# Waits behind groups of GpSimd scatters and gathers in a macaron block with a mixture of experts

## The reference

```python
def reference(x, ...):
    x = x + 0.5 * _L0_ffn_ref(_layernorm(x), ...)
    x = x + _L0_attn_ref(_layernorm(x), ...)
    x = x + 0.5 * _L0_ffn_ref(_layernorm(x), ...)
    return x

def _forward(x, ...):                       # the feed-forward step
    xn = (x - mu) * rsqrt(var + EPS) * ln_gamma + ln_beta
    abel_out = gelu(xn @ abel_w + abel_b)
    topw, topi = top_k(xn @ moe_gate_w + moe_gate_b, 2)      # 2 of 8 experts
    w_dense = sum(one_hot(topi, 8) * softmax(topw)[..., None], axis=-2)
    h = gelu(einsum('bsd,edh->ebsh', xn, ew1) + eb1)         # 128 -> 256
    moe_out = einsum('ebsd,bse->bsd', einsum(h, ew2) + eb2, w_dense)
    for i in range(3):
        moe_out = moe_out @ expm(gens[i])
    gate = sigmoid(concatenate([abel_out, moe_out]) @ gc_w + gc_b)
    return x + abel_out * (1.0 - gate) + moe_out * gate
```

## Time and profile before

| | |
|---|---|
| time, median of 3 runs | 788.86 us (786.06 to 794.77) |
| span of the profiled execution, first to last instruction | 883.8 us |
| TensorE busy | 683.1 us (77%) |
| VectorE busy | 568.2 us (64%) |
| GpSimd busy | 485.6 us (55%) |
| ScalarE busy | 410.8 us (46%) |
| mean granted TensorE clock | 0.913 |

### The profile page before, as it was taken

One profiled execution on the slowest core, in us unless ns is written; L12 is line 12 of the kernel. 1 busy time (PEld: TensorE's weight loads), 2 busy tenths in 40 slices (PEclk: granted clock), 3 DMA queues, 4 the chain that ended last, 5 costly groups with the idle time before them and its releaser, 6 DMA issues.

```text
span 883.8 us, 16149 instructions
## 1 busy us (share of the span) xinstructions
PE 683.1 (77%) x4719; PEld 492.3 (56%) x4719; DVE 568.2 (64%) x1922; ACT 410.8 (46%) x931; POOL 485.6 (55%) x588
## 2 busy tenths in 40 slices
PE   1465667979897798997988979999997777838760
PEld 1355656979793354654646545455544466837750
DVE  3675545968767876876767767787673235745538
ACT  2243411545560265664545645556554655615530
POOL 2656554034512666576866768373645466566661
PEclk9968777988898899998999999999997999969985
DMA  8614544744348313023050240302201235233525
GB/s 242 205 48 117 132 123 115 183 112 105 94 113 192 110 31 98 18 65 87 2 130 21 49 103 1 98 17 55 61 13 53 85 78 167 75 93 84 175 96 154
DMA packets 89825, 84.04 MB, mean 95 GB/s; under 512 B 14561, under 2 KB 72556, under 8 KB 89580
## 3 DMA queue, kind: packets, MB, share of 16 engines
q1 hardware_dynamic: 74472, 57.51, 25.8%
q0 software_dynamic: 8800, 19.72, 7.5%
q10 hardware_dynamic: 6468, 5.79, 2.8%
HBM read 43.84 MB, written 31.13 MB: 85 GB/s over the span
## 4 chain that ended last, share of the span: by engine, by line
PE 46%; DVE 15%; another core or an unknown queue 11%; issue 7%; ACT 7%; SPq 5%; ACTq 3%; DMA 3%; POOL 1%; DVEq 0%; POOLq 0%
PE bank L2361 6%; PE bank L2271 6%; PE bank L2401 6%; PE bank L2286 6%; PE bank L2426 6%; SPq L595 4%; DVE mx_of L1923 3%; PE pair L2449 2%; PE bank L2363 2%; ACT beside_parts L1254 2%; DMA qT<-mT_zero 2%; PE pair L2213 2%; PE bank L2246 1%; ACT arena L1326 1%
## 5 line engine op out<-in xcount | busy, mean ns | idle before, releaser
L1326 ACT ACTIVATE arena<-bank 128x512 f32<-128x512 f32 x320 | 184.0, 599 | 175.2 <-PE bank L2401 147.1
L1923 DVE TENSOR_REDUCE mx_of<-bank 128x4 f32<-128x512 f32 x320 | 204.2, 684 | 81.9 <-PE bank L2361 42.9
L2401 PE MATMUL bank<-qT,kZ 128*128 128x512 f32 (+3 forms) x512 | 156.9, 377 | 19.2 <-ACT arena L1326 12.4
L975 POOL TENSOR_SCALAR_AFFINE_SELECT arena<-arena 128x256 f32<-128x256 f32 (+1 forms) x192 | 95.4, 521 | 123.9 <-ACT arena L1326 122.5
L2361 PE MATMUL bank<-kZ,qT 128*128 128x512 f32 x320 | 148.5, 481 | 15.7 <-DVE mx_of L1923 6.2
L2401 PEld LDWEIGHTS bank<-qT,kZ 128*128 128x128 f32 x512 | 95.7, 197 | 49.2 <-ACT arena L1326 24.1
L868 POOL DMA_INDIRECT z_rows<-beside_kZ,place x80 | 78.7, 984 | 51.5 <-DVE place L1685 29.8
L2361 PEld LDWEIGHTS bank<-kZ,qT 128*128 128x128 f32 x320 | 63.1, 200 | 70.7 <-issue 31.4
L885 POOL DMA_INDIRECT sums<-y_rows,y_place x56 | 54.4, 971 | 84.9 <-DMA y_rows<-arena 70.0
L2426 PE MATMUL bank<-arena,vA 128*9 128x512 f32 (+3 forms) x1024 | 92.4, 440 | 5.2 <-POOL arena L975 2.7
L1254 ACT ACTIVATE beside_parts<-bank,hidden_bias 128x128 f32<-128x128 f32 x160 | 45.5, 381 | 69.6 <-remote 44.0
(11 more groups left out here) (286 smaller groups left out, 1306.7 us busy)
## 6 DMA issues: line engine op xcount, KB each, us to landing
arena<-z_rows SPq DMA_DIRECT2D x128, 66.0 KB
qT<-parts SPq DMA_DIRECT2D x42, 128.0 KB
kZ<-parts SPq DMA_DIRECT2D x168, 32.0 KB
y_rows<-arena SPq DMA_DIRECT2D x20, 264.0 KB, 3.3
kZ<-bias_k_r SPq DMA_DIRECT2D x8, 512.0 KB
beside_kZ<-y_rows SPq DMA_DIRECT2D x7, 528.0 KB, 3.9
z_rows<-in_spare SPq DMA_DIRECT2D x4, 528.0 KB
z_rows<-in_spare SPq DMA_DIRECT2D x32, 66.0 KB
```

What stands on the lines that cost most here:

```text
L975: g_.affine_select(out=cut, in_=cut, compare_op=ALU.is_ge, fill=0.0, base=0, pattern=[[0, 2], [0, blocks], [1, P]], channel_multiplier=-1) ...
L1326: a_(dst, src, ACT.Exp).then_inc(exp_ok.sem, 1)
L1923: v.tensor_reduce(mx_of[:, queries, :, t, keys], ps_a[n % NA][:, :].rearrange("p (q n) -> p q n", q=NQ), AX.X, ALU.max).then_inc(reduced.s ...
L2401: return mm(outp, kZ[u][:, h, lo:lo + P], qT[u][:, t, lo:SEQ], start=start, stop=True, skip_group_check=(kind != "full"))
```

## The change

In send_z, GpSimd counts the scatters of a chunk that it has issued. For the chunks of the set-up (g below 8) it waits after the third and after the sixth until all that were issued have landed. In gather, for the chunks 0 and 1 of layer 0, it waits after the second, fourth, sixth and eighth gather in the same way. Everything else is as it was.

```diff
+SET_UP_GROUP, EARLY_GROUP = 3, 2
...
             def send_z(g, picks=(0, 1), tiles=range(NT)):
                 run = run_of_chunk(*divmod(g, CH))
                 wait(pool, placed, g)
                 z_done(pool, g)
+                sent = 0
                 for k in picks:
                     for t in tiles:
                         g_.indirect_dma_start(z_rows[run], bass.IndirectOffsetOnAxis(place[g % DEEP][:, k, t:t + 1], 0),
                                               zz(g)[:, k, t, :], None).then_inc(z_sent[g % DEEP], 16)
+                        sent += 1
+                        if g < CH and sent % SET_UP_GROUP == 0:
+                            pool.wait_ge(z_sent[g % DEEP], 16 * sent)
...
+                got = 0
                 for k in picks:
                     for t in tiles:
                         g_.indirect_dma_start(terms(0, c)[0][:, t, k, :], None, y_rows[run],
                                               bass.IndirectOffsetOnAxis(y_place[:, c, k, t:t + 1], 0)
                                               ).then_inc(sums_in[1 if c == 1 else 0], 16)
+                        got += 1
+                        if c < 2 and got % EARLY_GROUP == 0:
+                            pool.wait_ge(sums_in[c], 16 * got)
```

## The result

| | before | changed |
|---|---|---|
| median of 4 runs | 788.52 us | 835.64 us |
| lowest to highest | 786.06 to 794.77 | 835.52 to 836.70 |
| ratio | 1 | 1.059, 95% interval 1.056 to 1.063 |
| span of the profiled execution | 883.8 us | 833.8 us |

The change makes the kernel 47 us slower, 5.9%. The profiled execution of the changed kernel took 835.52 us, 1.7 us more than its span. Taking a profile does not by itself add 95 us, then; whether the unchanged kernel does so whenever it is profiled is the question of e1. They answer to the earlier trace rows.

The account below looks back on a forecast made before the run. TensorE held 46% of the chain; 99 us of unknown waits were taken as mostly profile-only. Set-up 1.0, gathers 3.2, less 1.8 us saved, gave +2.4 us on 788.9: 791.3 us, range 770 to 804.

Parts of the forecast that it names:

- So in the profiled execution an engine can be held until GpSimd's pile of indirect DMAs has landed.: Set-up and gathers: idle VectorE and ScalarE restart about when the pile's last transfer lands; 99 us of unknown waits in all.
- what goes: Set-up, experts of layer 0, gathers: a tenth of the unknown waits is 3.7 us; shorter runs save half, 1.8 us.
- the holes are real in the timed runs too: Rival: unknown waits in set-up and gathers also exist unprofiled, so the change saves 17 us, 771.5 us; chance 0.33.
- The sign that the prediction had named for its reading: Whole kernel: unknown waits belong to the profile if the span falls by 10 us or more and the time does not.
- Set-up, the price of a wait, 1.45 us: GpSimd's scatters: each wait for landing adds 1.45 us over the 0.30 us gap, with ends 1.3 and 2.85 us.
- Set-up, the deadline: Before quad 6: scatters must land by 145.1 us in timed runs; they land 0.5 us late, taken as 1 us.
- the waits turn late: Rival: at 1.9 us a wait, quad 6 and both gathers' gates come late, 12.3 us together, 801.2 us; chance 0.31.
- Gathers: Chunks 0 and 1 of layer 0: chunk 0 costs about nothing, chunk 1 shows 3.2 us beyond ScalarE's slack.
- is not added twice: attention_norm(0): VectorE's wait for the roots, and TensorE's behind it, fall at about the gathers' 3.2 us, adding nothing.
- The Trainium skill's rule: DMA queues: engines serve both descriptor kinds round robin, so scatters hold nobody back and waits only cost, +4.2 us.

Follow-up runs that it names:

- e1: The kernel before, unchanged, profiled once more: ratio 1.0005, span 788.0 us.
- e7: Kernel before plus only the 16 set-up waits, with SyncE's key-row loads moved behind the loads of quads 6 to 14: 813.02 us, ratio 1.030.
- e3: Kernel before plus only the 8 waits of the gathers, none in the set-up: 801.25 us, ratio 1.017.
- e8: Kernel before plus only the four waits in chunk 1's gather: 795.8 us, ratio 1.011.
- e2: Kernel before plus only the 16 waits of the set-up, none in the gathers: 827.99 us, ratio 1.050.
- e5: Kernel before plus set-up waits only in the chunks 0 and 1 (4 of 16), none in the gathers: 791.9 us, ratio 1.003.

## Why the prediction was wrong

The forecast was 791.3 us, in a range to 804; 835.6 us were measured. Point by point:

- *"So in the profiled execution an engine can be held until GpSimd's pile of indirect DMAs has landed."* In the execution that it read, engines did restart as piles landed. Of the ten executions profiled later, e1 of the unchanged kernel among them, none has a wait for an unknown queue on the page's chain. The argument that most of these waits exist only while the profile is taken had the right consequence and the wrong reason, which was luck: profiling does not bring them, for e1 was profiled too. One execution was odd. What disturbed it stays open; no run repeated it. The term "what goes" is 0, not 1.8 us, and the rival *the holes are real in the timed runs too* falls with it. The sign that the prediction had named for its reading, a span that falls by 10 us or more and a time that does not, was met (883.8 to 833.8 us), but it only says that the first execution was odd.
- *Set-up, the price of a wait, 1.45 us.* This is the step that failed, with the largest error. The 1.45 us are near the price of a scatter that lands alone (1.57 us less 0.30, or 1.3). The mean of all 16 was 3.2 us, or 2.9 over the gap, and that of the twelve that count, in the chunks 2 to 7, was 3.6 us, or 3.3 over the gap, because scatters land behind SyncE's key rows (e7). The upper end of 2.85 us that the prediction kept from the earlier trace rows was about the mean of the 16 and below that of the twelve, and it was set aside as the less clean case.
- *Set-up, the deadline.* Taking 23 us of unknown waits off the set-up gave experts from 126 us. They start at 116.66 (e1), 32.4 us earlier than in the disturbed execution, so 9.4 us of the disturbance stood elsewhere than in the waits with no name. With quad 6 issued by 132.59, landed 1.75 us later and turned at 142.15, the slack was 7.8 us, close to the predicted 7.9, so the deadline is 126.91 + 7.8 = 134.7 and not 145.1.
- Put right, the prediction's own sum works: 62.81, six chunks of 10.2 us, 12 waits of 3.3 us over the gap, and a landing make 62.8 + 61.2 + 39.7 + 1.8 = 165.5. The gate opened at 165.54, 30.8 us behind 134.7, where the prediction had 0.5 us. Of these 30.3 us the price of the waits is 22.3, the deadline 10.4, and the landing 0.3; the earlier start at 62.8 instead of 65.5 takes 2.7 off. TensorE was ready for quad 6 1.1 us earlier than in e1 (176.03 - 34.95 = 141.08 against 142.15), issuing from the gate on took 0.9 us less (4.7 against 5.7), and quad 6 was turned 5.75 us after its loads were issued instead of the 1.75 us reckoned: 30.8 + 1.1 - 0.9 + 4.0 = 35.0, the 34.95 us. The lower clock behind the wait adds 1.6 us, for which the prediction had no term. The mechanism of the rival *the waits turn late* was the right one. Its price of 1.9 us a wait and its 801.2 us were too small.
- *Gathers.* Expected 3.2 us; measured 11 (e3). The slacks of 4.3 and 2.2 us came from subtracting ScalarE's holes from a disturbed timeline. In the clean one ScalarE waits 0.23 us already, and chunk 0's waits show from the first on: its gate is 5.0 us later than in e1. A wait between gathers took 1.8 to 3.2 us in e3 and not 1.75. The prediction held that VectorE's wait for the roots "is not added twice", and so dropped the term that was larger: 6.75 us at attention_norm(0) in e3 and 8.24 us in e8, of which 1.98 us were there before.
- *The Trainium skill's rule* (DMA: Bandwidth & Descriptors, SWDGE vs HWDGE vs iDMA), that the two kinds of descriptors sit in different queues of a DMA engine and are served in turn, gives, in the prediction's working, a sum without a gain, +4.2 us. The runs agree that nothing is gained by letting the pile land; the taking of turns itself they do not show. What they do show is that scatters land later beside SyncE's key rows: 1.5 us a wait on average (e2 against e7).

## What to carry to other kernels

Before reckoning with slack from a profile, hold its span against the timed runs: 883.8 against 788.9 us meant that the timeline was not that of a usual execution, and slack read from it (4 us of idle time before each chunk) was not there; subtracting the strange waits did not give back the clean timeline, a second profile did. A wait until an indirect DMA has landed cost at least 1.57 us, and behind bulk loads up to 8.22 us, so it belongs only where the issuing engine idles anyway (e5: four waits for under 3 us; with the twelve further on, 38 us). And ask which transfer is the last that a later stage needs: here one quad load needed all scatters, so every delay in their queue beyond 7.8 us of slack came out at the end at full price.

## What the runs showed of the hardware

- A wait for an indirect scatter took at least 1.57 us from the end of its instruction in the changed kernel (1.56 in e7); behind two loads of key rows of 0.5 MB each the wait for three scatters took 8.22 us.
- The 48 scatters of the chunks 2 to 7 issue at 1.27 us apart with no wait for earlier ones to land (e1): GpSimd's idle time between them is its 0.3 us gap throughout.
- TensorE stood idle for 34.95 us before quad 6 in the changed kernel. Its granted clock was 0.50 of full speed (1.2 GHz) from 146 to 179 us, 0.96 from 179 to 182 and 1.00 (2.4 GHz) from 182 to 191; in e1, without the wait, it was 1.00 from 142 to 151. Four transposes of a quad took 1.11 us at the low clock and 0.60 at full speed.
- One execution of 883.8 us in span, in which idle engines restarted 1.54 and 1.56 us after the end of a run of scatters, stands against 57 timed runs of the same kernel between 785.9 and 800.1 us.
